# FFN2 of an AdaLN block with quantized FFN: five folded positions in place of three, partial results copied by ScalarE

## Reference

```
h0  = relu(concat(x, mean(x), hidden) @ W + b)      # hidden comes from cond_512
h1  = relu(quant(h0) @ quant(w1) + b1)              # 512 -> 2048  (FFN1)
y   = quant(h1) @ quant(w2) + b2                    # 2048 -> 512  (FFN2)
out = x + y
```

## Time and profile before

| | us |
|---|---|
| median of 3 runs | 321.23 (320.97 to 321.96) |
| profiled execution, its own time | 321.04 |
| span of the profiled execution | 319.2 |
| TensorE busy | 310.8 |
| VectorE busy | 272.4 |
| ScalarE busy | 200.7 |
| GpSimd busy | 115.0 |

### The profile page before, as it was taken

The page is one execution under the profiler, slowest core; times in us unless marked ns, Lnnn a source line. Parts: engine busy times, 40 slices in busy tenths (PEclk is TensorE's granted clock), DMA queues, the critical chain, the costliest instruction groups (busy, mean ns, idle before and its releaser), DMA issues.

```text
span 319.2 us, 4733 instructions
## 1 busy us (share of the span) xinstructions
PE 310.8 (97%) x1635; PEld 193.3 (61%) x1635; DVE 272.4 (85%) x602; ACT 200.7 (63%) x356; POOL 115.0 (36%) x96
## 2 busy tenths in 40 slices
PE   6999999999999999999999999999999999999995
PEld 6868888888776544444444444444458548647844
DVE  1699988997986699999999999999999698698855
ACT  2435775597386995466665664089959759677400
POOL 1066425634540599992180000710603301400410
PEclk9999999999999999999999999999999999999999
DMA  7999999999973379896990060060999996957952
GB/s 224 205 243 232 226 222 237 259 225 374 282 172 66 70 263 50 342 423 254 424 415 37 6 223 37 35 230 1 367 361 418 408 405 225 402 192 259 341 215 99
DMA packets 51624, 75.57 MB, mean 237 GB/s; under 512 B 20344, under 2 KB 34960, under 8 KB 46864
## 3 DMA queue, kind: packets, MB, share of 16 engines
q1 hardware_dynamic: 51408, 74.99, 78.2%
q10 hardware_dynamic: 192, 0.28, 0.5%
HBM read 45.89 MB, written 25.17 MB: 223 GB/s over the span
## 4 chain that ended last, share of the span: by engine, by line
PE 81%; DVE 11%; DMA 3%; issue 2%; SPq 2%; DVEq 0%
PE bank L589 24%; PE bank L714 21%; PE bank L816 15%; PE bank L826 11%; PE bank L686 6%; DMA x_in<-in_x_dram 3%; DVE hidden L1190 2%; PE bank L701 2%; DVE bank L1320 1%; DVE hidden L1051 1%; DVE bank L1315 1%; DVE hidden L1344 1%; DVE hidden L1342 1%; DVE hidden L1346 1%; DVE hidden L1347 1%
## 5 line engine op out<-in xcount | busy, mean ns | idle before, releaser
L816 PE MATMUL bank<-w_t 128*128 128x512 f16 (+1 forms) x272 | 55.9, 366 | 0.0
L1190 DVE TENSOR_SCALAR_CACHE_REDUCE hidden<-bank,qb,hmax 128x512 f32<-128x512 f32 x62 | 47.6, 806 | 6.4 <-PE bank L714 3.8
L494 POOL TENSOR_TENSOR x_lo<-hidden,x_hi 128x512 fp32r<-128x512 f32 x28 | 35.4, 1303 | 45.6 <-ACT x_hi L910 45.6
L589 PE MATMUL bank<-x_hi,cw_hi 128*128 128x512 f32 x128 | 48.4, 393 | 0.8 <-DVE hidden L1056 0.7
L589 PE MATMUL bank<-x_lo,cw_hi 128*128 128x512 f32 x128 | 48.4, 390 | 0.0
L589 PE MATMUL bank<-x_hi,cw_lo 128*128 128x512 f32 x128 | 48.4, 389 | 0.0
L570 POOL TENSOR_TENSOR pool_r<-pool_r,steps 128x512 f32<-128x512 f32 x16 | 20.2, 1274 | 75.3 <-DVE steps L1367 59.7
L1210 DVE CUSTOM_DVE_ANT_0 hidden<-hidden,bank,hmax 128x512 f32<-128x512 f32 x66 | 45.9, 743 | 0.2
L816 PEld LDWEIGHTS bank<-w_t 128*128 128x128 f16 x272 | 26.6, 98 | 28.3
L1016 ACT ACTIVATE pool_q<-hidden,s_quant 128x512 uint8<-128x512 f32 x63 | 39.1, 710 | 5.2 <-PE bank L826 4.9
L1016 ACT ACTIVATE w_t<-hidden,s_quant 128x512 uint8<-128x512 f32 x56 | 34.7, 709 | 11.7 <-PE bank L816 11.7
(11 more groups left out here) (157 smaller groups left out, 506.2 us busy)
## 6 DMA issues: line engine op xcount, KB each, us to landing
hidden_spill<-hidden SPq DMA_DIRECT2D x16, 1024.0 KB, 9.9
hidden<-hidden_spill SPq DMA_DIRECT2D x16, 1024.0 KB, 10.9
x_in<-in_x_dram SPq DMA_DIRECT2D x32, 256.0 KB, 7.1
pool_r<-in_x_dram SPq DMA_DIRECT2D x8, 1024.0 KB, 5.5
pool_q<-in_L_ffn_w_dram SPq DMA_DIRECT2D x7, 1024.0 KB, 10.2
out_dram<-pool_r SPq DMA_DIRECT2D x7, 1024.0 KB, 8.6
pool_r<-in_L_cond_W_dram SPq DMA_DIRECT2D x2, 1024.0 KB, 9.9
x_in<-in_L_ffn_w_dram SPq DMA_DIRECT2D x1, 1024.0 KB, 5.4
```

Of the source, the lines that this page charges most:

```text
L494: pool.tensor_tensor(x_lo[:, n % 2, k, :], x_t[:, k, :], x_hi[:, n % 2, k, :].bitcast(F32), ALU.subtract).then_inc(lo_ready, 1)
L589: return pe.matmul(REL[ot][:, :], w[:, k, ot * P:(ot + 1) * P], v[:, n % 2, k, :], start=(k == 0 and w is cw_hi and v is x_hi), stop=(k == ...
L816: return pe.matmul(y_bank[:, cols], hid_q[n % 2][:, ft, j * P:(j + 1) * P], w2_t[:, ft, cols], start=(ft == 0), stop=(ft == FT - 1))
L1190: dve.tensor_scalar(hidden[:, at:at + TB], y_bank[:, :], qb1[:, ft:ft + 1], hmax[:, ft:ft + 1], ALU.add, ALU.max, accum_out=hmax[:, ft:ft ...
```

## The change

Positions 5 and 7 are folded too, so that 2, 4, 5, 6 and 7 are folded and 0, 1 and 3 plain. Since folded positions now follow each other, the sums `HS` and the kept rows get a second place (in a slot of `hidden`), for odd positions. Position 7's values go to slot 2, and its reload waits for one position more and comes later in SyncE's queue, after reuse(2). The six copies of a folded position go to ScalarE (`keep`, placed between the roundings of the next position's tiles). VectorE now adds the bias in the bank to products 1a, 1b, 5a and 5b (`bias`). For 5a and 5b it adds the difference of two halves of the bias (`b2_over`), so that the outputs c21 need no bias of their own, only a scaling. The order of products and takes changes. Half of the f16 sums of the next position is formed inside the present one. GpSimd's additions wait for those sums where the next position is folded. In position 7 only rows 0 and 2 go over GpSimd; the four last quarter tiles are added to x by VectorE and stored one by one.

```diff
-        FOLDED = (2, 4, 6)
-        SLOT = (0, 1, 2, 3, 1, 2, 3, 1)
+        FOLDED = (2, 4, 5, 6, 7)
+        SLOT = (0, 1, 2, 3, 1, 2, 3, 2)
-        F1, F5, F2, FV = (bank[0], bank[3]), bank[1], bank[2], bank[7]
+        F1, F2, F5, FV = (bank[0], bank[3]), (bank[2], bank[5]), bank[1], bank[7]
+        PRODUCTS = ("1a", "1b", "2a", "5a", "6a", "3a", "7a", "5b", "4a", "6b", "3b", "7b", "2b", "4b")
+        KEEPS = ("k1a", "k1b", "k5a", "kxa", "k5b", "kxb")
+        TAKES = ("b1a", "b1b", "c11a", "m11a", "b5a", "c12a", "m12a", "c22a", "m22a", "b5b", "m21a", "c12b", "m12b",
+                 "c22b", "m22b", "c11b", "m11b", "m21b")
...
-                    sp.wait_ge(hid_ready, tiles_to({5: 3, 6: 4, 7: 5}[n]))
+                    sp.wait_ge(hid_ready, tiles_to({5: 3, 6: 4, 7: 6}[n]))
...
-            reload(SLOTS + 3)
             store(2)
             reuse(2)
+            reload(SLOTS + 3)
...
+                        if n + 1 in FOLDED:
+                            pool.wait_ge(hs_ready, 8 * FOLDED.index(n + 1) + (4 if r < 2 else 8))
...
                 part2(0, a11, B11, F1[0], start=True)
+                if n != FOLDED[0]:
+                    pe.wait_ge(fold_taken, takes_to(n))
+                part2(1, a11, B11, F1[1], start=True)
+                part2(0, a12, B21, F2[0], start=True)
                 pe.wait_ge(hs_ready, sums + 5)
+                part2(0, hs[0], W2S[0], F5, start=True)
+                pe.wait_ge(fold_kept, keeps_to(n, "k1a"))
                 pe.wait_ge(hs_ready, sums + 6)
+                part2(0, hs[1], W2S[1], F1[0])
+                pe.wait_ge(fold_kept, keeps_to(n, "k5a"))
                 pe.wait_ge(hs_ready, sums + 7)
+                part2(0, hs[3], B22, F5)
+                pe.wait_ge(fold_kept, keeps_to(n, "kxa"))
                 pe.wait_ge(hs_ready, sums + 8)
+                part2(0, hs[2], W2S[2], F1[0])
+                pe.wait_ge(fold_taken, takes_to(n, "m12a"))
+                part2(1, hs[0], W2S[0], F5, start=True)
                 pe.wait_ge(fold_taken, takes_to(n, "c22a"))
                 part2(0, a22, W2S[3], F1[0])
...
+            def keep(n, name, product, row, cols, r):
+                if product[0] == "6":
+                    act.wait_ge(fold_done, products_to(n, product))
+                else:
+                    act.wait_ge(fold_taken, takes_to(n, "b" + product))
+                act.activation(OUT_ROWS[n % 2][:, row, cols], r[:, FIRST], ACT.Copy).then_inc(fold_kept, 1)
...
+                if rounded == 2:
...
+                    keep(n, "k1a", "1a", 0, FIRST, F1[0])
+                elif rounded == 4:
+                    keep(n, "k1b", "1b", 1, FIRST, F1[1])
+                elif rounded == 5:
+                    keep(n, "k5a", "5a", 2, LAST, F5)
+                    keep(n, "kxa", "6a", 0, LAST, F1[0])
+                elif rounded == 9:
+                    keep(n, "k5b", "5b", 3, LAST, F5)
+                elif rounded == 11:
+                    keep(n, "kxb", "6b", 1, LAST, F1[1])
...
+                if not plain:
+                    sums12(n, 1)
+                bias(n, "1a", F1[0], b2_b[:, FIRST])
+                if not plain:
+                    sums43(n, 1)
+                elif two:
                     add_bias(n - 1, 2)
+                bias(n, "1b", F1[1], b2_b[:, FIRST])
                 if two:
                     scale_y(n - 1, 2)
+                    add_x(n - 1, 2)
+                elif plain:
                     add_bias(n - 1, 3)
+                result(n, "c11a", "2a", 0, FIRST, F2[0], F2[0], "k1a")
+                bias(n, "5a", F5, b2_over)
...
+                result(n, "c12a", "3a", 0, LAST, F5, F5, "kxa")
+                result(n, "c22a", "7a", 2, LAST, F1[0], FV, "k5a")
+                bias(n, "5b", F5, b2_over)
...
+                if n + 1 in FOLDED:
+                    sums12(n + 1, 0)
+                dve.wait_ge(fold_done, products_to(n, "4a"))
+                scale_row(n, 2, FIRST, F1[0])
+                if n + 1 in FOLDED:
+                    sums43(n + 1, 0)
+                result(n, "c12b", "3b", 1, LAST, F5, F5, "kxb")
+                result(n, "c22b", "7b", 3, LAST, F1[1], FV, "k5b")
+                result(n, "c11b", "2b", 1, FIRST, F2[1], F2[1], "k1b")
+                dve.wait_ge(fold_done, products_to(n, "4b"))
+                scale_row(n, 3, FIRST, F1[1])
```

More of the change, by code:

```diff
@@ L293, in adaln_quantized_ffn @@
         ROWS = {n: (0, 2, 1, 3) if n in FOLDED else (0, 1, 2, 3) for n in BY_POOL}
+        ROWS[NB - 1] = (0, 2)
         FIRST = slice(0, HALF)
         LAST = slice(HALF, TB)
-        F1, F5, F2, FV = (bank[0], bank[3]), bank[1], bank[2], bank[7]
-        PRODUCTS = ("1a", "5a", "6a", "3a", "7a", "2a", "1b", "4a", "5b", "6b", "3b", "7b", "2b", "4b")
-        TAKES = ("k1a", "k5a", "kxa", "c12a", "m12a", "c22a", "m22a", "c11a", "m11a", "k1b", "c21a", "m21a", "k5b",
-                 "kxb", "c12b", "m12b", "c22b", "m22b", "c11b", "m11b", "c21b", "m21b")
@@ L304, in adaln_quantized_ffn, with rows_to @@
-        ROW_TAKES = ("m11a", "m21a", "m11b", "m21b")
+        F1, F2, F5, FV = (bank[0], bank[3]), (bank[2], bank[5]), bank[1], bank[7]
+        ROWS_OWNER = {n: max([m for m in BY_POOL if m < n and m % 2 == n % 2], default=None) for n in FOLDED}
+        def rows_to(n, row=None):
+            return sum(len(ROWS[m]) for m in BY_POOL[:BY_POOL.index(n)]) + (ROWS[n].index(row) + 1 if row is not None else 0)
+        PRODUCTS = ("1a", "1b", "2a", "5a", "6a", "3a", "7a", "5b", "4a", "6b", "3b", "7b", "2b", "4b")
@@ L861, in folded @@
-                pe.wait_ge(fold_taken, takes_to(n, "m11a"))
-                part2(1, a12, B21, F2, start=True)
+                pe.wait_ge(fold_kept, keeps_to(n, "k1b"))
+                part2(1, hs[1], W2S[1], F1[1])
+                pe.wait_ge(fold_kept, keeps_to(n, "k5b"))
+                part2(1, hs[3], B22, F5)
+                pe.wait_ge(fold_kept, keeps_to(n, "kxb"))
+                part2(1, hs[2], W2S[2], F1[1])
+                if n - 1 in PLAIN:
+                    pe.wait_ge(y_taken, plain_to(n - 1, 2))
@@ L863, in folded @@
+                part2(1, a12, B21, F2[1], start=True)
                 pe.wait_ge(fold_taken, takes_to(n, "c22b"))
@@ L875, in _ @@
                         mm.then_inc(y_done, 1)
-            for n in range(1, NB - 1):
+            for n in range(1, NB):
                 if n in FOLDED:
@@ L1018, in _ @@
                                    ACT.Copy, scale=s_quant[:, ft:ft + 1]).then_inc(hid_ready, 1)
+                    if n - 1 in FOLDED:
+                        keeps(n - 1, i + 1)
+            for i in range(FT):
+                keeps(NB - 1, i + 1)
         @block.vector
@@ new lines, in scale_row @@
+            def scale_row(n, row, cols, r):
+                if n == NB - 1 and row not in ROWS[n]:
+                    at = (SLOTS - 1) * WC + row * D + cols.start
+                    xs = x_res[:, at:at + HALF]
+                    dve.tensor_tensor(r[:, FIRST], r[:, FIRST], s2_b[:, cols], ALU.mult).then_inc(fold_taken, 1)
+                    name = [m for m, j, c in LAST_PIECES if (j, c) == (row, cols)][0]
+                    dve.wait_ge(fold_taken, takes_to(n, name))
+                    dve.wait_ge(xres_landed[1], 16 * SLOTS)
+                    dve.tensor_tensor(xs, xs, r[:, FIRST], ALU.add).then_inc(last_added, 1)
+                    return
+                dve.tensor_tensor(OUT_ROWS[n % 2][:, row, cols], r[:, FIRST], s2_b[:, cols], ALU.mult
+                                  ).then_inc(fold_taken, 1)
@@ L1375, in finish_folded @@
                 if two:
                     scale_y(n - 1, 2)
-                else:
+                    add_x(n - 1, 2)
+                elif plain:
                     add_bias(n - 1, 3)
-                keep("6a", 0, LAST, F1[0])
-                if two:
-                    add_x(n - 1, 2)
-                result("c12a", "3a", 0, LAST, F5, F5, "kxa")
-                result("c22a", "7a", 2, LAST, F1[0], FV, "k5a")
-                result("c11a", "2a", 0, FIRST, F2, F2, "k1a")
-                keep("1b", 1, FIRST, F1[1])
+                result(n, "c11a", "2a", 0, FIRST, F2[0], F2[0], "k1a")
@@ L1393, in finish_folded @@
                     scale_y(n - 1, 3)
-                else:
+                if plain:
                     add_x(n - 1, 3)
-                keep("6b", 1, LAST, F1[1])
-                if two:
-                    add_x(n - 1, 3)
-                result("c12b", "3b", 1, LAST, F5, F5, "kxb")
-                result("c22b", "7b", 3, LAST, F1[1], FV, "k5b")
-                result("c11b", "2b", 1, FIRST, F2, F2, "k1b")
-                result("c21b", "4b", 3, FIRST, F1[1], F1[1])
+                if n + 1 in FOLDED:
+                    sums12(n + 1, 0)
```

160 lines of the change are left out of this document (75 added, 85 removed).

## The result

The changed kernel takes 327.9 us, the median of 4 runs (326.1 to 330.96), against 321.1 us (320.95 to 321.96) for the kernel before: the ratio is 1.0218, interval 1.0146 to 1.0289. It is slower, by 1.5 to 2.9% by these runs. The profiled run took 326.1 us, with a span of 324.3. Measured again, in 6 runs, it took 326.31 us (325.9 to 330.17), ratio 1.0165 (1.0119 to 1.021). A few runs are some 2 to 5 us longer at a mean granted clock of 0.992 to 0.995 (4 of 63 of the kernel before; 2 of 10 of the changed one, 330.17 and 330.96), so the medians of 4 and 6 runs are loose.

A forecast was written before the change was run, and what follows sets the result against it. TensorE was taken to set the pace, with little slack on VectorE. Position changes of +1.53, +1.53, +0.37, +1.48 and -0.15 plus +0.42 at the end gave +5.2 on 321.23: 326.4 us, range 324.3 to 328.6.

The forecast's parts named there:

- 3a: TensorE's product 3a in folded positions, waiting for ScalarE's copy after VectorE's bias 5a: 0.60 to 1.18 us late.
- 5b: TensorE's product 5b, directly after 7a, waits for m12a, which reads bank F5: 0.28 us late in every folded position.
- 4b: TensorE's product 4b waits for c22b in VectorE's queue: 0.89 us late in position 4, 0.29 in position 5.
- The 0.06 before 7b: TensorE's product 7b was to wait 0.06 us for the copy kxb.
- the path 5a, bias, copy, 3a: Handover from product 5a to 3a with both queues free: 1.14 us against 0.87 of cover, at least 0.27 late.
- The disputed cost: ScalarE's 256-wide copy from PSUM to SBUF: taken as 0.40 us, 0.32 from start to start.
- At 10.9 there are 3 us to spare: Position 7's reload, issued about 278.5 and wanted at 292.6: 3 us spare landing in 10.9, costing 0.9 at 15.0.
- that sign of being wrong: A gap on TensorE before position 7 ended by a DMA would show the prediction wrong.
- TensorE as the bound: Rival: all waits hidden, -3.8 us on TensorE and +0.6 at the end, 318.0 us; chance 4%.
- ScalarE as the bound: Rival: ScalarE sets the pace, with the copy near 0.69 us: 330 us; chance 5%.
- only the direct paths bite: Rival: no queueing, only 0.27 + 0.28 us in each folded position, 12.77 a position: 320.8 us; chance 5%.
- The clock: Rival: the clock falls; one position at 1.2 GHz costs another 12.2 us, giving 338 us; chance 2%.

The follow-up runs named there:

- e4: Changed kernel without the reload of position 7, with VectorE adding bias 5a ahead of c11a and m11a: 324.53 us.
- e7: Kernel of e6 with ScalarE's copies k5a and kxa behind tile 4 instead of 5, k5b behind tile 10 instead of 9: 321.71 us.
- e5: Changed kernel without the reload of position 7, with result c12a put in bank 6 instead of F5: 325.13 us.
- e6: Changed kernel without the reload of position 7, with both bias 5a early and c12a in bank 6: 322.76 us.
- The edits together: Bias 5a early, c12a in bank 6 and ScalarE's copies moved, on the changed kernel without the reload of position 7: 321.71 us.
- e8: Changed kernel with position 5 plain again and the reload of position 7 issued ahead of reuse(2): 324.86 us.
- e11: Changed kernel with all three edits, the reload of position 7 in quarters, and GpSimd adding x to position 7's c12b and c22b: 320.92 us.
- e2: Changed kernel without the reload of position 7, which is computed from old values: 325.91 us.
- e3: Changed kernel with the reload of position 7 issued ahead of reuse(2), nothing left out: 326.17 us.
- e12: Changed kernel with only the reload of position 7 altered, issued in quarters ahead of reuse(2): 326.62 us.
- the best version: The kernel of e11, with all three edits, the quartered reload and GpSimd's two additions: 320.92 us.
- e1: The changed kernel run again, unaltered: 326.31 us.

## Why the prediction was right

**The sum.** Forecast was +5.2 on the span, by the stretch alone. Measured is 324.3 - 319.2 = +5.1: the stretch grew by 85.13 - 80.30 = 4.83, position 2 started 0.17 later, and the last store took 0.1 more. By position, forecast and measured: 2: 13.75 and 13.64; 3: 13.82 and 13.81; 4: 14.05 and 13.97; 5: 14.18 and 14.10; 6: 14.00 and 13.94; 7: 13.67 and 13.63; VectorE's end after TensorE's: 2.01 and 322.06 - 320.02 = 2.04. Small slips of addition in the prediction (position 5's terms give 14.17, not 14.18, and the upper end is 328.7, not 328.6) change nothing.

**The stalls by name.** 3a was forecast late by 1.18, 0.60, 1.14, 0.96, 0.96 (positions 2, 4, 5, 6, 7). The starts show 1.12, 0.52, 1.07, 0.92, 0.90. 5b: 0.28 each, as forecast. 4b in positions 4 to 7: 0.89, 0.29, 0.29, 0.20 forecast, 0.91, 0.32, 0.32, 0.21 measured. Positions 6 and 7 were to start 0.18 late and start 0.20 and 0.19 late. The 0.06 before 7b is not there. Measured that is 4.5 us before 3a, 1.4 before 5b, 1.8 before 4b and 0.4 at the starts, 8.1 in all, and with 0.45 more at the end it turns the 3.7 us by which the five positions would be shorter without any wait (3.8 forecast) into 4.8 lost.

Of the 4.5 us before 3a, experiment e4 shows 1.9 to be VectorE's queue and e7 about 1.3 ScalarE's order; some 1.3 stay, 0.23 to 0.34 a position, where the prediction gave 0.27 as the least for the path 5a, bias, copy, 3a. Experiment e5 shows that 5b waits for m12a, and e6 that the two stalls add up. The edits together take 4.66 of the 4.83 us back. 4b waits for c22b behind VectorE's other work. The edits leave that as it is, but e8 moves the wait of 0.74 us with that work from position 4 to 6, and in e11, with less for VectorE to do, the 0.2 of position 7 is gone.

**The disputed cost.** The copy was taken at 0.40 and 0.32 from start to start. It is 0.375 to 0.380, and 0.26 to 0.28 from start to start. Every folded position came out 0.04 to 0.11 below the forecast, since 3a is 0.04 to 0.08 less late and 7b is not late. The shorter copy fits both, though no experiment changed it alone.

**Where the prediction was off.** "At 10.9 there are 3 us to spare" for the reload: the landing of the last transfer was 13.7 us after its issue at 279.9, at 293.66, 1 us after ScalarE wanted it. The prediction counted all four transfers from the first issue, near 278.5; the last is issued 1.4 us later, so even 10.9 would have left only 1.8. And "at 15.0 it costs 0.9" was wrong in its mechanism too: ScalarE has idle time ahead of copy k1a that takes up such a delay (e2, e3 and e12 have the same stretch to 0.03). TensorE had no gap before position 7 that a DMA ended, so that sign of being wrong did not show. The forecast 326.4 is met by the profiled run (326.1) and the repeat (326.31), while the first median of four, 327.9, is 1.5 higher. It lies in the forecast range, but by luck: that part of the range was left for a slow copy and a late reload, and neither cost anything. One run of 328.87, at a clock of 0.998, is not explained. What makes runs of 1 to 3 us more at a clock near 1.00 stays open; the starts of position 2 (236.65 to 238.14) show that part of it lies ahead of FFN2.

**The rivals.** TensorE as the bound, at 318.0, did not come about: it is busy for 12.6 to 12.9 us in folded positions of 13.6 to 14.1. ScalarE as the bound needed a copy near 0.69 us; it took 0.38, and e7 shows ScalarE with room. That only the direct paths bite (12.77 a position) needed VectorE idle when 5a ends, and it was not: bias 5a started at 282.90 for a product done at 281.84. The clock stayed at 1.00 in every stretch from position 2 on, with a gap of 0.5 to 1.1 us before each of the five products 3a. The Trainium skill's rule in "TensorE: Matmul & The Clock Gate", section "A second HAM failure mode: psum-queue depth-cycling", did not show here: these stretches stay at the upper level. All profiled executions have a mean granted clock of 0.997 or more, so this says nothing of others.

## What to carry to other kernels

When the bounding engine gets less to do, list for each of its waits the queue that the awaited instruction stands in and the work written ahead of it, and walk that forward: here 3.7 us saved on TensorE turned into 4.8 us lost without any engine being short of time on average. Then look at what is left as well: 4b's waits and the direct path to 3a kept the best version level with the kernel before. A handover over two engines (bias on VectorE, then copy on ScalarE) needs more than one product of cover (here about 1.1 us against 0.87), so put as many independent products between as the handover lasts, and put the instruction that starts it first in its queue. And compare variants by a stretch of the profile that begins after the unrelated noise: it repeated to 0.03 us between single profiled runs, where medians of 6 runs were off by 0.6 (e5). It does not see what happens outside it.

## What was not expected of the hardware

Copies of 128x256 f32 from PSUM to SBUF on ScalarE take 0.375 us and start 0.27 us after one another, less than the estimate from wider ones (0.40 and 0.32). The stretch of 85 us repeated to 0.03 us in four profiled runs besides the first (85.13, 85.13, 85.12, 85.10 in e1, e2, e3 and e12), while whole runs of the changed kernel at a clock of 0.997 or more lay from 325.9 to 328.87. Of the four reloads of 1 MB, issued one behind the other, the last landed 11.9 us after its issue in e3, and 13.7 in the changed kernel, where the load of x, 1 MB, was issued ahead of them.
